# Running decays of a state-space scan brought to all partitions by one bf16 product for four heads

## What is computed

```python
A_disc = -jnp.exp(A_log)[None, None, :] * dt
A_cs = jnp.cumsum(A, axis=-1)                       # within a chunk, for each head
Lmat = jnp.minimum(jnp.exp(segsum(A)), EXP_CLAMP)   # exp(A_cs[l] - A_cs[s]) for l >= s
Y_diag = jnp.einsum('bclhn,bcshn,bhcls,bcshp->bclhp', Cm, Bm, Lmat, X)
states = jnp.einsum('bclhn,bhcl,bclhp->bchpn', Bm, decay_states, X)
Y_off = jnp.einsum('bclhn,bchpn,bhcl->bclhp', Cm, inter, jnp.exp(A_cs))
```

## Time and profile before

| | us |
|---|---|
| median of 3 runs | 3973.22 (3966.16 to 3978.81) |
| the profiled execution's own time | 3973.28 |
| its span | 3971.5 |
| TensorE busy | 3450.7 (87%), mean granted clock 0.914 |
| VectorE busy | 2610.3 (66%) |
| ScalarE busy | 1180.8 (30%) |
| GpSimd busy | 503.4 (13%) |

### The profile page before, as it was taken

The page is one execution under the profiler, slowest core; times in us unless marked ns, Lnnn a source line. Parts: engine busy times, 40 slices in busy tenths (PEclk is TensorE's granted clock), DMA queues, the critical chain, the costliest instruction groups (busy, mean ns, idle before and its releaser), DMA issues.

```text
span 3971.5 us, 37643 instructions
## 1 busy us (share of the span) xinstructions
PE 3450.7 (87%) x12941; PEld 2128.7 (54%) x12941; DVE 2610.3 (66%) x3732; ACT 1180.8 (30%) x1948; POOL 503.4 (13%) x404
## 2 busy tenths in 40 slices
PE   1877878878879999999999589998989898989998
PEld 0553553553555776777777346543554356434643
DVE  5877877877875777888888244664466435644563
ACT  1332332332331544333433132212222223123210
POOL 1002003003003111111111201110212011201100
PEclk9979989989989999999999797899789978998799
DMA  3202201201203878788787500231013201220011
GB/s 137 80 28 46 80 30 46 81 29 34 73 29 123 274 239 262 228 272 264 254 277 242 219 37 1 85 120 65 32 75 111 85 32 75 100 97 32 2 63 42
DMA packets 276638, 436.71 MB, mean 110 GB/s; under 512 B 52320, under 2 KB 189536, under 8 KB 263904
## 3 DMA queue, kind: packets, MB, share of 16 engines
q1 hardware_dynamic: 256768, 379.84, 28.9%
q0 software_dynamic: 19680, 54.46, 4.2%
HBM read 364.59 MB, written 93.77 MB: 115 GB/s over the span
## 4 chain that ended last, share of the span: by engine, by line
PE 61%; DVE 23%; DVEq 6%; ACT 4%; issue 2%; DMA 2%; POOL 1%; SPq 0%; ACTq 0%; POOLq 0%
PE bank L1012 11%; PE bank L1041 6%; PE bank L1283 6%; PE bank L1296 4%; PE bank L1304 4%; PE bank L1212 4%; PE bank L828 3%; PE bank L1149 3%; DVE sb_gla L1884 3%; PE bank L1190 2%; DVE sb_ratio L1859 2%; DVEq L1865 2%; PE bank L1018 2%; PE bank L1248 1%; PE bank L808 1%
## 5 line engine op out<-in xcount | busy, mean ns | idle before, releaser
L1012 PE MATMUL bank<-sb_xT,sb_work 128*128 128x256 f32 x2304 | 513.0, 382 | 1.6 <-issue 0.8
L1012 PEld LDWEIGHTS bank<-sb_xT,sb_work 128*128 128x128 f32 x2304 | 439.3, 192 | 75.2 <-issue 17.5
L828 PE MATMUL bank<-sb_gla,sb_work 128*128 128x256 f32 x896 | 260.3, 443 | 112.6 <-DVE sb_work L1886 100.0
L1041 PE MATMUL bank<-sb_work,sb_hT 128*128 128x512 f32 (+1 forms) x666 | 296.1, 592 | 0.0
L828 PEld LDWEIGHTS bank<-sb_gla,sb_work 128*128 128x128 f32 x896 | 188.9, 218 | 175.6 <-DVE sb_work L1886 121.1
L808 PE MATMUL bank<-sb_hT,sb_work 128*128 128x512 f32 x384 | 181.1, 620 | 99.6 <-DVE sb_hT L1833 99.6
L1296 PE MATMUL bank<-sb_parts,sb_gla 128*128 128x512 f32 x512 | 240.3, 613 | 4.5 <-ACT sb_gla L1628 4.5
L1304 PE MATMUL bank<-sb_parts,sb_gla 128*128 128x512 f32 x512 | 230.8, 593 | 5.9 <-DVE sb_work L2450 5.9
L1283 PE MATMUL bank<-sb_work,sb_parts 128*128 128x512 f32 x512 | 230.8, 610 | 2.8 <-ACT sb_work L1641 2.8
L1884 DVE TENSOR_TENSOR sb_gla<-sb_gla,sb_work 128x1024 f32<-128x1024 f32 x112 | 146.0, 1303 | 128.9 <-PE bank L828 122.9
L1149 PE MATMUL bank<-sb_parts,sb_hT 128*128 128x512 f32 x512 | 228.7, 605 | 0.0
(11 more groups left out here) (396 smaller groups left out, 6103.3 us busy)
## 6 DMA issues: line engine op xcount, KB each, us to landing
sb_work<-scratch_gu SPq DMA_DIRECT2D x63, 1408.0 KB, 7.5
sb_parts<-scratch_mx SPq DMA_DIRECT2D x16, 3072.0 KB, 12.1
sb_work<-moe_w SPq DMA_DIRECT2D x63, 512.0 KB, 6.7
scratch_y<-sb_work SPq DMA_DIRECT2D x48, 512.0 KB, 7.8
sb_parts<-scratch_fq SPq DMA_DIRECT2D x24, 1024.0 KB, 8.0
sb_work<-w_qkvg SPq DMA_DIRECT2D x64, 256.0 KB, 2.5
scratch_gu<-moe_w SPq DMA_DIRECT2D x32, 512.0 KB, 5.8
sb_parts<-fT SPq DMA_DIRECT2D x48, 256.0 KB, 3.4
```

Of the source, the lines that this page charges most:

```text
L828: mm = pe.matmul(dst.rearrange("p (h n l) -> p h n l", h=HPC, l=size), kS[u % 2][:, k * P:(k + 1) * P], late[:, :, k, :, 1, :], start=True ...
L1012: mm = pe.matmul(dst, egu[j % 3][:, which * NC + k, m * P:(m + 1) * P], xt[j % 2][:, k, :], start=(k == 0), stop=(k == NC - 1))
L1041: mm = pe.matmul(bank(YB[s]), einter[j % 2][0:n, a:a + P], edn[j % 3][0:n, m * D:(m + 1) * D], start=(m == 0), stop=(m == EC - 1))
```

## The change

The decays of 16 heads are written once for each image as three bf16 parts, whose sum is the fp32 value. Part `n` stands on partitions 32n to 32n+15 of `cs3`, for each head four times along the free dimension, masked so that only the copy `h % 4` is not zero. A broadcast is then one bf16 product with 96 rows, a matrix `sel4` of ones and zeros that chooses the group as weights, and 512 moving columns (four heads by 128 tokens). The semaphore `s_gm` goes, and `s_cst` at the end of the new work stands in its place. The table of constants grows by 8 columns.

```diff
@@ constant_table
+    row = np.arange(P)
+    parts["every4"] = ((row[:, None] % 32 < SH) & (row[:, None] % 4 == np.arange(4))).astype(np.float32)
+    parts["four"] = ((row[:, None] % 32 // 4) == np.arange(SH // 4)).astype(np.float32)
@@ names of tiles in sb_gla
+        cs3 = gla[0:96, 0:4 * T // 2].bitcast(BF16).rearrange("p (a t) -> p a t", a=4)
+        csr, csh = gla[0:SH, 1024:1024 + T], gla[0:SH, 1024 + T:1024 + T + T // 2].bitcast(BF16)
+        sel4 = gla[0:96, 5376:5376 + 2 * P].bitcast(BF16).rearrange("p (g m) -> p g m", g=4)
@@ TensorE, after the projections of an image
                 pe.wait_ge(s_silu.sem, s_silu.at(b, NT * 4))
-                pe.wait_ge(s_gm.sem, s_gm.at(b, 1))
+                pe.wait_ge(s_cst.sem, s_cst.at(b, 1))
...
                 def cs_bcast(k, g):
 
-                    for hh in range(4):
-                        h = g * 4 + hh
-                        mm = pe.matmul(bank(5 + g % 2)[:, hh * P:(hh + 1) * P], idn[0:SH, h:h + 1].to_broadcast([SH, P]),
-                                       cst_[:, k * P:(k + 1) * P], start=True, stop=True)
-                    mm.then_inc(s_csb.sem, 1)
+                    pe.matmul(bank(5 + g % 2), sel4[:, g, :], cs3[:, :, k * P:(k + 1) * P],
+                              start=True, stop=True).then_inc(s_csb.sem, 1)
@@ VectorE, after the masked products Gm
-                tt(Gm[:, :, :], r3(bank(5), P), cst("tri").unsqueeze(1).to_broadcast([P, NT, P]), ALU.mult)\
-                    .then_inc(s_gm.sem, 1)
+                tt(Gm[:, :, :], r3(bank(5), P), cst("tri").unsqueeze(1).to_broadcast([P, NT, P]), ALU.mult)
+
+                dve.memset(gla[0:96, 0:4 * T // 2], 0.0)
+                if b == 0:
+                    dve.tensor_copy(sel4, cst("four", 96).unsqueeze(2).to_broadcast([96, 4, P]))
+                dve.tensor_copy(csh, cst_)
+                dve.drain()
+                for n in range(3):
+                    q = tt(cs3[32 * n:32 * n + SH], csh.unsqueeze(1).to_broadcast([SH, 4, T]),
+                           bcast(cst("every4", SH), T), ALU.mult)
+                    if n < 2:
+                        tt(csr, csr if n else cst_, csh, ALU.subtract)
+                        dve.drain()
+                        dve.tensor_copy(csh, csr)
+                        dve.drain()
+                q.then_inc(s_cst.sem, 1)
+                dve.drain()
                 dve.wait_ge(s_exps.sem, s_exps.at(b, 1))
```

More of the change, by code:

```diff
@@ L347, in build @@
         s_raw, s_sq, s_th, s_ln, s_rms, s_ea, s_sin, s_exps = series("s_set_act", 8)
-        s_v, s_dt, s_cs, s_ang, s_bcn, s_rope, s_tmc, s_gm = series("s_set_dve", 8)
+        s_v, s_dt, s_cs, s_ang, s_bcn, s_rope, s_tmc, s_cst = series("s_set_dve", 8)
         s_xz = ev("s_xz", NT * 4)
```

## The result

The changed kernel takes 3944.7 us (median of 5 runs, 3934.45 to 3947.74) against 3973.22 (5 runs, 3966.16 to 3978.81). The ratio is 0.9925, with a 95% interval of 0.9911 to 0.9939: 0.75% faster, 28.5 us. The forecast was 3945, in a range of 3928 to 3964. The profiled execution spans 3942.0 us, 29.5 less than before.

A forecast was written before the change was run, and what follows sets the result against it. TensorE was taken to bound the stretch from a tile's first broadcast to its output projection, with ScalarE close behind. Shorter work 8.6 + 5.5 + 4.2 = 18.3 us, plus 10 for the clock, took 3973.3 to 3945 us, range 3928 to 3964.

The forecast's parts named there:

- What bounds a head: From a tile's first broadcast to its output projection: TensorE ends last before, ScalarE's copy after; 3.00 us instead of 4.08.
- The product: Each broadcast as one bf16 product: at most 0.43 us apart, 0.59 start to end; the skill's estimate was 0.22.
- Tiles 2 and 3: Eight stretches from first broadcast to output projection, each 1.08 us shorter: gain 8.6 us.
- Tile 1: Four stretches from first broadcast to output projection, limited by ScalarE's table load, each 1.37 us shorter: gain 5.5 us.
- Tile 0: No output projection here; VectorE starts 0.56 us earlier and the fourth broadcast gives 0.49, in four images: 4.2 us.
- The fourth broadcast: In tiles 1 to 3 it lies under VectorE's work that diagonal(1) waits for anyway: costs and gains nothing.
- The setup: VectorE's new work per image, 12.3 us, hidden under the rest of the x and z projections: costs nothing.
- The clock: Six of twelve output projections ran slow at half clock; most falls go: 10 us, between 0 and 15.2.
- The clock gives nothing: Rival, chance 0.20: clock falls go after some heads and come after others, no clock gain; 3955 us.
- The clock gives more: Rival, chance 0.18: all six falls go and one more stretch per image stays at full clock; 3928 us.
- the clock falling in every head: Rival, chance 0.04: half clock also in the six heads that keep full clock, and shifted copies; 4014 us.
- The next in line takes half: Rival, chance 0.10: TensorE waits for ScalarE's chain, leaving half of 18.3 us and no clock help; 3964 us.

The follow-up runs named there:

- the setup alone: The changed kernel with the old broadcast of four fp32 16-row products, new setup and semaphore kept but unused: 3974.4 us, ratio 0.9994 to the old kernel.
- the three setups: The changed kernel with VectorE's new setup done three times in a row: 4010.0 us, 65.3 more than the change.
- long heads: The changed kernel with each broadcast's bf16 product done five times over: 3957.0 us with 96 rows, 3993.7 with 16.
- the fillers: The changed kernel plus unread bf16 products of 512 columns where TensorE waits: 3877.4 us with 96 rows, 3953.4 with 16.

## Why the prediction was right

- *What bounds a head.* Right. TensorE ended last before, ScalarE's copy does now, and TensorE waits. The forecast had 3.00 us and 0.7 us idle for tiles 2 and 3; measured are 2.80 and 1.10.
- *The product.* I took the upper bound, 0.43 us apart and 0.59 from start to end. It is 0.22 and 0.38. The estimate from the Trainium skill (TensorE: Matmul & The Clock Gate, section Back-to-back issue gap) was right, and the bound from the fp32 row was twice as much.
- *Tiles 2 and 3.* 8.6 us forecast, 11.0 measured (33.4 us of heads before, 22.4 after). The difference is the product (1.7 us) and the two heads of image 1 that were longer than 4.08.
- *Tile 1.* 5.5 forecast, 3.7 measured: 3.58 us instead of 3.04. (The three terms as I wrote them add up to 2829.47 and not 2829.53, which would have made it 5.7.) The step that failed was to take ScalarE's table load at a fixed distance from the head's start. In image 2 ScalarE's scaling began 1.06 us ahead of the head before, and 0.54 us ahead of it after (2815.10 against 2815.64). The shifted copies, which had run partly at half clock, had become quicker (4.07 us to 3.54 up to the head), ScalarE's chain had not, and TensorE now waits for it. These 0.52 us are the whole difference between 3.04 and 3.58, within 0.02.
- *Tile 0.* 4.2 forecast, 5.4 measured.
- *The work's sum.* 18.3 forecast, 20.2 measured (14.8 + 5.4), of which 2.5 are the clock's share in the old heads.
- *The fourth broadcast* gains nothing in tiles 1 to 3, as forecast: in the change `diagonal(1)` still waits for VectorE, 1.24 us.
- *The setup.* 12.3 us forecast, 10.5 in image 2, hidden. Shown by the setup alone (0.9994) and by the three setups, which TensorE waited for as soon as they were longer than the cover of 19.6 to 21.3 us.
- *The clock.* 10 us chosen between 0 and 15.2; all 15.2 came in the profile. The 10 was a choice and not a calculation, and the 15.2 hangs on a profile that happened to have six slow projections; the execution with the setup alone had two. With the 2.5 us in the old heads and the 2.7 us lost behind the output projections the clock's share of the stage is 15.0. The reason given had two halves. "Shorter" is right: with one 16-row product the falls go as well. "96 rows" is right as a mechanism (3957.0 against 3993.7 us with long heads) but isn't what this change needs.
- *The total* hit 3945 to 0.3 us, and that is luck: the stage gained 35.0 us instead of 28.3, the profiled execution lost 5.5 outside it, and tiles 2 and 3 and the clock gave more than forecast where tile 1 gave less. The median moved by 28.5.
- *The rivals.* *The clock gives nothing:* no, 15 us, though its mechanism, falls that come elsewhere, took 2.7. *The clock gives more:* no, what is left of the stage beside the heads, tile 0 and the six falls became 0.3 us longer. The product as slow as fp32, the setup uncovered, the clock falling in every head: none of them. *The next in line takes half:* in part. ScalarE took 1.8 us of tile 1's gain, not half of the sum. What I had not seen is how much the clock still costs in the rest of the tile: 67 us, which no part of the change touches.

## What to carry over

A stretch in which TensorE waits, or has only products of few rows, can cost more than its own length, since the clock can fall for what follows. So look at the granted clock by stretch and not at the busy share. Where such a wait is there anyway, products into a free bank with 96 rows kept most of the clock here and gave more than twice what the change gave; with 16 rows they gave nothing. And when a step gets shorter, ask which engine's chain now ends last, measured from where that chain starts and not from where the step starts.

## What the runs showed of the hardware that I had not expected

- Rows count for the clock. Two kernels with the same number of products, the same columns and the same durations at full clock (1.24 and 1.25 us for five) differ by 36.7 us with 16 or 96 rows in the broadcast, and by 76 us with 16 or 96 rows in the fillers. The Trainium skill (TensorE: Matmul & The Clock Gate, section What's actually happening) says that the clock follows how busy TensorE has been. The runs go further: with the same products in the same places it follows how many rows they take, too.
- The clock fell with no gap in TensorE's work and stayed up over gaps of 1.10 and 1.39 us with a short head. Before, in image 1, TensorE was busy for all 6.50 us from 2397.0 to 2403.5 at a granted clock of 1.00, and from 2404 on the clock was 0.50. What it did in between was shifted copies, 16-row broadcasts and transposes.
- How many falls an execution has is not fixed: six slow output projections in the kernel before, two in the same work with the setup added.
- A bf16 product of 512 columns takes 377 to 381 ns alone with 96 rows and 374 with 16. Rows don't change its duration, but each change between 16 and 128 rows took about 0.1 us more.
